# Expert pieces and convolution products in another order in the first and last steps, and no discarded products behind the first projection

## The reference

```python
x = x + _L0_conv_ref(_gn(x), g1, w_qkv, mem_kv, w_out, b_out, g2)
x = x + _L1_conv_ref(_gn(x), expert_weight, rconv_w, rconv_b, fc_w, fc_b)
```

## Time and profile before

| | us |
|---|---|
| median of the runs | 445.23 |
| the profiled execution | 443.4 |
| its span | 441.7 |
| TensorE busy | 417.4 (95%) |
| VectorE (DVE) busy | 350.1 (79%) |
| ScalarE (ACT) busy | 295.5 (67%) |
| GpSimd (POOL) busy | 264.9 (60%) |
| mean granted TensorE clock | 0.995 |

### The profile page before, as it was taken

The page is one execution under the profiler, slowest core; times in us unless marked ns, Lnnn a source line. Parts: engine busy times, 40 slices in busy tenths (PEclk is TensorE's granted clock), DMA queues, the critical chain, the costliest instruction groups (busy, mean ns, idle before and its releaser), DMA issues.

```text
span 441.7 us, 8932 instructions
## 1 busy us (share of the span) xinstructions
PE 417.4 (95%) x2638; PEld 368.5 (83%) x2638; DVE 350.1 (79%) x769; ACT 295.5 (67%) x907; POOL 264.9 (60%) x249
## 2 busy tenths in 40 slices
PE   7798898999999999999999999999999999999796
PEld 6698796989898988889887989888888989788585
DVE  3474989797989899797989798998979696967710
ACT  2766867868676868678676868686786868544221
POOL 4745648567584849396775849394956756424130
PEclk9999999999999999999999999999999999999899
DMA  6420242316262443515162524425161525242331
GB/s 190 181 96 2 95 192 96 131 62 237 98 235 98 159 176 125 211 45 229 64 240 95 219 113 148 185 96 236 42 229 62 192 95 192 95 174 113 158 128 47
DMA packets 18787, 61.63 MB, mean 140 GB/s; under 512 B 2992, under 2 KB 4032, under 8 KB 18752
## 3 DMA queue, kind: packets, MB, share of 16 engines
q1 hardware_dynamic: 18752, 61.21, 36.6%
HBM read 19.29 MB, written 8.39 MB: 63 GB/s over the span
## 4 chain that ended last, share of the span: by engine, by line
PE 48%; DVE 22%; issue 16%; ACT 10%; DMA 1%; POOL 1%; DVEq 1%; ACTq 0%; SPq 0%; POOLq 0%
PE ps_conv L1255 15%; PE ps_y L1200 6%; PE ps_att L1167 6%; DVE w_full L1006 4%; ACT expert_raw L655 4%; DVE y_scaled L894 3%; PE ps_y L1206 3%; PE ps_y L1190 3%; DVE route_terms L960 3%; ACT qk L594 3%; DVE q_exp L846 2%; PE ps_qkv L1146 2%; PE ps_qkv L1147 2%; PE ps_qkv L1148 2%; PE ps_stat L1213 2%
## 5 line engine op out<-in xcount | busy, mean ns | idle before, releaser
L594 ACT ACTIVATE qk<-ps_qkv,scale 128x256 f32<-128x256 f32 x128 | 55.5, 472 | 5.6 <-PE ps_qkv L1148 3.4
L537 POOL TENSOR_TENSOR left_hi<-zeros 128x32 fp32r<-128x32 f32 x16 | 7.5, 469 | 78.6 <-DMA right_lo<-img_lo 78.6
L661 ACT ACTIVATE w_hi<-w_full 128x1152 fp32r<-128x1152 f32 x16 | 18.7, 1168 | 51.1 <-DVE w_full L1012 51.1
L530 POOL TENSOR_TENSOR w_lo<-w_full,w_hi 128x1152 fp32r<-128x1152 f32 x16 | 42.8, 2675 | 11.2 <-ACT w_hi L661 6.2
L485 POOL TENSOR_TENSOR x_lo<-x,x_hi 128x1024 fp32r<-128x1024 f32 x16 | 38.4, 2400 | 14.4 <-ACT x_hi L584 14.4
L511 POOL TENSOR_TENSOR scale<-ssq,minus_half 128x8 f32<-128x8 f32 x16 | 26.2, 1639 | 32.5 <-DVE ssq L887 32.5
L1146 PE MATMUL ps_qkv<-wqk_hi,x_hi 128*128 128x256 f32 x128 | 40.8, 319 | 2.4 <-ACT x_nt L575 1.3
L635 ACT ACTIVATE y_scaled<-ps_y 128x128 f32<-128x128 f32 x128 | 33.5, 293 | 14.0 <-PE ps_y L1200 14.0
L1255 PE MATMUL ps_conv<-left_lo,w_hi 128*128 128x512 f32 (+1 forms) x96 | 39.1, 407 | 0.0
L1255 PE MATMUL ps_conv<-right_hi,w_lo 128*128 128x512 f32 (+1 forms) x96 | 38.5, 401 | 0.0
L1255 PE MATMUL ps_conv<-right_lo,w_hi 128*128 128x512 f32 (+1 forms) x96 | 37.9, 395 | 0.0
(11 more groups left out here) (152 smaller groups left out, 1333.9 us busy)
## 6 DMA issues: line engine op xcount, KB each, us to landing
xa<-in_x_dram SPq DMA_DIRECT2D x16, 512.0 KB, 4.0
xb<-in_x_dram SPq DMA_DIRECT2D x16, 512.0 KB, 4.6
out_dram<-expert_raw SPq DMA_DIRECT2D x16, 512.0 KB, 2.9
left_hi<-img_hi SPq DMA_DIRECT2D x16, 511.5 KB, 2.9
right_hi<-img_hi SPq DMA_DIRECT2D x16, 511.5 KB, 3.7
left_lo<-img_lo SPq DMA_DIRECT2D x16, 511.5 KB, 2.9
right_lo<-img_lo SPq DMA_DIRECT2D x16, 511.5 KB, 3.7
expert_raw<-_conv_expert_weight_dram SPq DMA_DIRECT2D x1, 1728.0 KB, 9.2
```

Source lines behind the costliest of these rows:

```text
L530: nc.gpsimd.tensor_tensor(w_lo[p][:, :, :].rearrange("p t o -> p (t o)"), w_full[:, :], w_hi[p][:, :, :].bitcast(F32).rearrange("p t o -> ...
L594: nc.scalar.activation(qk[:, t, :], ps_qkv[t % 2][:, 0:QK], ACT.Copy, scale=scale1[:, t:t + 1]).then_inc(qkv_done, 1)
```

## The change

Four things differ. `keep_busy` and its 126 products go, and `constants` issues two discarded products instead of four. The expert pieces go to other places in the lists of TensorE and ACT. The convolution of samples 1 to 14 goes by tap (three parts of one tap, then the next tap), with the waits for `w_lo`, `img_lo` and the borders before its first product, while samples 0 and 15 go by pass as before. And `conv_at` draws 4 products ahead of their place in step 4 and 12 in step 18.

```diff
@@ ACT step
                 do(results, t, p, 5, 0)
+                once(expert_evacuate, t, 2, 0)
+                once(expert_evacuate, t, 2, 1)
+                once(expert_evacuate, t, 2, 2)
+                once(expert_evacuate, t, 2, 3)
                 once(expert_evacuate, t, 3, 6)
-                once(expert_evacuate, t, 2, 3)
-                once(expert_evacuate, t, 2, 4)
+                once(expert_evacuate, t, 3, 7)
...
                 do(results, t, p, 5, 1)
+                once(expert_evacuate, t, 2, 4)
                 once(expert_evacuate, t, 2, 5)
                 do(k_x_evacuate, t, p, 2)
                 do(x_copy, t, p, 1, 1)
                 do(x_k_evacuate, t, p, 2)
-                once(expert_evacuate, t, 3, 7)
+                once(expert_evacuate, t, 3, 8)
                 do(q_evacuate, t, p, 2, 0)
                 do(qkv_evacuate, t, p, 1, 0)
-                once(expert_evacuate, t, 3, 8)
...
-                once(expert_evacuate, t, 1, 0)
                 do(squares2, t, p, 2)
-                once(expert_evacuate, t, 1, 1)
-                once(expert_evacuate, t, 1, 2)
@@ TensorE constants
-                discarded(4)
+                discarded(2)
@@ TensorE convolution
+                by_pass = isinstance(b, int) and b in (0, B - 1)
+                if by_pass:
+                    products = [(n, part) for part in range(3) for n in range(TAPS)]
+                else:
+                    products = [(n, part) for n in range(TAPS) for part in range(3)]
+                    pe.wait_ge(w_lo_done, b + 1)
+                    pe.wait_ge(img_lo_done, b + 1)
+                    pe.wait_ge(edges_done, b + 1)
                 for h in range(2):
                     if past(b, 1):
                         pe.wait_ge(result_done, 2 * (b - 1) + h + 1)
-                    for pass_ in range(3):
+                    for n, part in products:
@@ TensorE step
+                def conv_at(at, n):
+                    if isinstance(t, int) and t == at:
+                        conv(n)
...
                 conv(1)
-                once(expert_transpose, t, 2, 6)
                 conv(3)
-                once(expert_transpose, t, 3, 8)
                 conv(2)
-                keep_busy(t, "key_contexts")
                 do(key_contexts, t, p, 2)
...
                 do(key_context_transpose, t, p, 2)
+                conv_at(OLDEST + B - 2, 3)
                 turn(group_means, t, p, 0)
...
                 conv(1)
+                conv_at(OLDEST + B - 2, 5)
+                conv_at(OLDEST, 4)
                 if not isinstance(t, int) or t != 1:
                     turn(group_variances, t, p, 0)
...
-                once(expert_transpose, t, 1, 0)
-                once(expert_transpose, t, 1, 1)
                 do(outputs, t, p, 2)
-                once(expert_transpose, t, 1, 2)
+                conv_at(OLDEST + B - 2, 4)
                 do(routing, t, p, 3)
...
-                once(expert_transpose, t, 1, 3)
                 conv(6)
-                keep_busy(t, "project")
+                once(expert_transpose, t, 2, 6)
                 do(project, t, p, 1, 6)
                 conv(1)
                 do(project, t, p, 1, 7)
+                once(expert_transpose, t, 1, 0)
+                once(expert_transpose, t, 1, 1)
                 conv(5)
+                conv(1)
+                conv(14)
+                once(expert_transpose, t, 1, 2)
+                once(expert_transpose, t, 1, 3)
+                once(expert_transpose, t, 2, 7)
+                do(x_transpose, t, p, 0, 0)
+                do(x_transpose, t, p, 0, 1)
+                do(k_part_transpose, t, p, 1)
+                conv(8)
+                do(k_shift, t, p, 1)
+                once(expert_transpose, t, 2, 8)
                 once(expert_transpose, t, 1, 4)
                 once(expert_transpose, t, 1, 5)
...
                 do(y_transpose, t, p, 2)
                 conv(3)
```

More of the change, by code:

```diff
@@ L1237, in convolution @@
                         pe.wait_ge(result_done, 2 * (b - 1) + h + 1)
-                    for pass_ in range(3):
-                        if h == 0 and pass_ == 0:
+                    for n, part in products:
+                        if n == 0 and part == 0 and h == 0:
                             pe.wait_ge(w_hi_done, b + 1)
                             pe.wait_ge(img_hi_done, b + 1)
-                        if h == 0 and pass_ == 1:
+                        if by_pass and n == 0 and part == 1 and h == 0:
@@ L1243, in convolution @@
                             pe.wait_ge(img_lo_done, b + 1)
-                        if h == 0 and pass_ == 2:
+                        if by_pass and n == 0 and part == 2 and h == 0:
                             pe.wait_ge(w_lo_done, b + 1)
[L1246 to L1259, removed]
@@ new lines, in convolution @@
+                        if by_pass and n == KW and part == 0 and h == 0:
+                            pe.wait_ge(edges_done, b + 1)
+                        tap = TAP_ORDER[n]
+                        down = tap // KW - 1
+                        top, bottom = max(HH * h, -down), min(HH * (h + 1), H - down)
+                        hi, lo = ((left_hi, left_lo), (img_hi, img_lo), (right_hi, right_lo))[tap % KW]
+                        into = ps_conv[h][:, W * (top - HH * h):W * (bottom - HH * h)]
@@ L1261, in step @@
+                        weight, pixels = ((w_hi[p], hi[p]), (w_hi[p], lo[p]), (w_lo[p], hi[p]))[part]
+                        last = mm(into, weight[:, tap, :], pixels[:, top + down:bottom + down, :],
+                                  start=(n == 0 and part == 0), stop=(n == TAPS - 1 and part == 2))
+                        if n == TAPS - 1 and part == 2:
+                            last.then_inc(conv_ps, 1)
+                        yield
             def step(t, p):
@@ L1311, in step @@
                 do(project, t, p, 1, 7)
+                once(expert_transpose, t, 1, 0)
+                once(expert_transpose, t, 1, 1)
                 conv(5)
+                conv(1)
[9 more added lines that the diff above has]
+                once(expert_transpose, t, 2, 8)
                 once(expert_transpose, t, 1, 4)
                 once(expert_transpose, t, 1, 5)
[L1315 to L1324, removed]
-                do(k_shift, t, p, 1)
-                keep_busy(t, "y_transpose")
                 do(y_transpose, t, p, 2)
```

## The result

| | before | after |
|---|---|---|
| median of 15 runs each, side by side | 444.16 us (441.41 to 446.77) | 447.00 us (444.83 to 448.53) |
| ratio after / before, 95% interval | | 1.0052 [1.0030, 1.0073] |
| profiled execution, its own time | 443.40 us | 446.32 us |
| its span | 441.7 us | 444.6 us |
| its mean granted clock | 0.995 | 0.962 |

The change made the kernel slower by half a per cent, 2.3 us by the ratio. The forecast was 446.9 us.

The account below looks back on a forecast made before the run. TensorE, busy 95% of the span, was taken as the main bound, with DVE and ACT bounding parts. Terms -1.3 - 0.3 - 0.2 + 4.4 + 0.3 + 0.7 - 1.9 = +1.7 gave a median of 446.9 us, range 442.8 to 450.5.

Parts of the forecast that it names:

- pieces: First projection: moving three expert evacuations off ACT between the fourth and fifth projection tile ends it sooner, -1.3 us.
- discarded products: Constants: two fewer let the x transposes of sample 0 start sooner, gain ending at ACT's squares; -0.3 us.
- third step: ACT in the warm-up: one big expert evacuation leaves the place between x_k_evacuate and q_evacuate; -0.2 us.
- the clock: Warm-up: without idle products TensorE's granted clock falls and slows the work behind; +4.4 us, bounds 0 and 8.8.
- by tap: Samples 1 to 14: first convolution product waits for w_lo in two or three steps; +0.3 us, bounds 0 and 2.0.
- step 4: Four convolution products pulled ahead of group_variances and mixing, where TensorE is the bound; +0.7 us, bounds 0.2 and 0.9.
- the last step: From 407.7 us: 12 products fill TensorE's waits and avoid the clock fall, despite a w_lo wait; -1.9 us.
- All three stretches: Warm-up, 22.6 to 29.6, 42.5 to 49.6 and 64.0 to 70.5 us: become quiet; falls cost 1.6, 1.6, 1.2 us.
- The clock mostly holds: Warm-up rival: remaining real products keep the clock up, sum -2.7 to +0.1 us, likeliest 443.7 us; chance 0.22.
- Slow level lasts: Warm-up rival: low-clock spells last twice as long, 8.0 us for the three, giving 450.5 us; chance 0.15.
- w_lo late in every step: Loop rival: w_lo ends last in each step, costing 3.9 us instead of 0.3, giving 450.5 us; chance 0.05.
- No gain from reordering: First projection and last step rival: their -3.2 us shrinks to about -1, giving 449.1 us; chance 0.08.

Follow-up runs that it names:

- the fourth set: Kernel before without the 39 idle products ahead of project 6 (steps 2 and 3) and the x transposes of step 3; ratio 1.0012.
- the combined kernel: Kernel before with expert transposes and evacuations moved and 12 convolution products pulled ahead in step 18, all by pass, idle products kept; 439.96 us, ratio 0.9928.
- the second stretch: Kernel before without the 18 idle products between the x transposes of step 2 and the key contexts of sample 1; ratio 1.0037.
- the first stretch: Kernel before without the 38 idle products between the first x transposes of step 1 and the key contexts of sample 0; ratio 1.0046.
- the pieces: Kernel before with only the change's order of expert transposes and evacuations, 115 idle products kept, all by pass, four discarded; 442.83 us, ratio 0.9959.
- third: Kernel before without the 31 idle products between the x transposes of step 3 and the first convolution product; ratio 1.0030.

## Why the prediction was right

*The sum.* It gave +1.7 on the profiled execution; the profiled execution after is 446.32, +2.9. The ratio says +2.3. That 446.9 and the measured 447.0 lie so close has luck in it: the forecast added 1.8 us for the distance to a median of 445.23 from three runs, and with 15 that median was 444.16. Errors of the terms cancelled as well. In the traces the start gave 0.7 where the forecast had 1.8 (pieces, discarded products, third step), the clock cost 5.3 for 4.4, the loop gave back 0.7 where by tap was to cost 0.3, and step 4 and the last step came out as forecast.

*Clock.* The heaviest term, and the one with the sign. All three stretches fell, as the quiet stretch of before had let one expect. That it fell in the one profiled execution was partly luck, for in three other traces it doesn't (last section). Forecast +4.4, measured +4.75 and 4.8 by the two ways of taking the products out. The parts were 1.6, 1.6 and 1.2 by forecast, 2.0, 1.6 and 1.3 by medians. In the trace of the change they are 2.2, 2.3 and 0.8. The first covers most of the 16 key-context products (3.37 us for 1.95) and the work up to 33 us. The third costs 0.8 us here, 0.5 in the kernel with all idle products out, and 2.0 where it alone was quiet. It goes with how much of the spell is left behind y_transpose of sample 1, where TensorE is the bound: the clock is back 2.9, 2.5 and 5.5 us behind the start of that y_transpose. The Trainium skill (TensorE: Matmul & The Clock Gate, section "HAM oscillation — how this bites in real kernels") says that the cost is paid again at each quiet gap. The trace agrees for these three; the gap before 413 us fell in six traces and not in three, and the fourth set shows dips that cost 0.5 us at most, for there another engine is the bound.

*Pieces.* Forecast -1.3 and, with the third step, -1.5. Measured -1.8 with an interval of 1.1 to either side, and -1.21 at the key contexts in the combined kernel's trace, where both executions ran the projection at the full level. In the change ACT's fifth tile starts 0.35 us behind the end of the fourth, as said. In the change's own trace only -0.68 is left; its x transposes ran at the low level (0.93 us longer), and so they did in the change with the idle products back, which has -0.49. The -0.2 for ACT's third step was a term too many: in the combined kernel's trace outputs of sample 1 are 0.15 us further ahead (-1.21 to -1.36), and y_transpose of sample 1 is back at -1.25.

*Discarded products.* Forecast -0.3, measured between -1.3 and +1.5. This stays open; it is below what these runs can tell.

*By tap.* Forecast +0.3 with 2.0 as its end. There is one wait, 0.19 us, in the loop besides sample 14's 0.9, which the last step's term held. The loop as a whole gained 0.7 us in the trace of the change. By tap isn't needed for it: with all samples by pass the kernels of the second stretch and of the projection gain 0.7 and 1.0 us over the same steps, and by tap alone gains 0.2. In the change nearly all of it comes between the y_transposes of samples 5 and 6 (+5.42 to +4.68), where DVE waits for the input of a later sample, in before and in the change:

```profile
178.50 1.29 DVE L744 BATCH_NORM_STATS2 stats<-xa 128x6 f32<-128x512 f32 x2 [2.29 <-DMA xa<-in_x_dram]
183.12 1.28 DVE L744 BATCH_NORM_STATS2 stats<-xa 128x6 f32<-128x512 f32 x2 [1.50 <-DMA xa<-in_x_dram]
```

The work behind it in DVE's list, y_scaled included, shifts with it. The other traces follow this wait: with 2.1 to 2.4 us of it the offset of that step moves by at most 0.14, with 2.62 and 2.77 it grows by 0.25 and 0.47, and with 0.9 or less it shrinks by 0.7. So this is a matter of when a transfer lands in an execution, and what sets that wasn't tried. The forecast had no term for it.

*Step 4.* Forecast +0.7, found +0.73 at the outputs of sample 2, and 0.8 in the change with the idle products back. Whether it reaches the end stays open (above).

*Last step.* Forecast -1.9 in all; from y_transpose of sample 15 to the first product of sample 15 the offset goes from +4.73 to +2.81: -1.92. Its inner numbers hold too: routing 0.95 later by forecast, 0.93 in the trace; the wait for w_lo 1, found 0.90; for w_hi 1.5, found 1.36. But 1.6 of the 1.92 is the fall that the trace of before happened to have; against the two traces that have the last step of before and no fall, the term is -0.3.

*The rivals.* "The clock mostly holds" fell with the first page after. "Slow level lasts" was part right: in each of the kernels with one stretch quiet the low level lasts some 6.9 us, twice the 3.4 us at 413, and up to 13.6 us in the change. But the prices stay under twice the 1.6 (2.8, 2.1 and 2.0 us in those traces), and all three together cost 5.3 us in the change and 5.7 with all idle products out, where this rival had 8.0. "w_lo late in every step" fell with the by-tap kernel. "No gain from reordering" fell with the idle products put back. A gain was within reach (-0.6% with the idle products back), so the change is slower by the clock alone.

## What to carry to other kernels

Products that compute nothing can carry the clock: before taking them out, find for each stretch which engine is the bound behind it, because a fall cost 1.3 to 2.8 us where TensorE is (three of four sets here) and at most 0.5 us where it isn't. Fill a wait of TensorE with real products only where it waits anyway: in the last step, by pass, this gave 1.2 us beside the fall that was gone, and in step 4, without such waits, it put the outputs 0.7 us back. Before a single trace is the witness for a fall, look at a second one. A change with parts of both signs is worth splitting: all in all it was +2.3 us, and its two gaining parts alone are -3.2.

## What the runs showed of the hardware

*The level at the start differs between executions of one program.* In the profiled executions of before and of the combined kernel the x transposes and the first projection ran at the full level. In the change's, the low level covers 9 to 16 us (rows at the top), and the key contexts of sample 0 start 0.5 us later than in the combined kernel. In those of the kernels without idle products, by tap, of two discarded products, without the first stretch and without the projection's it lies on the first projection, and the key contexts of sample 0 come 2.8 to 3.0 us late. It lies there too in those of the pieces and of the change without step 4. The pieces and the combined kernel are the same code up to step 18, and their key contexts of sample 0 start 2.2 us apart. The stretch in the kernel without idle products:

```profile
16.00:22.00 6.00, 4.91 (x23) 0.53 0.00 1
```

By tap changes nothing before 80 us and has this too, so it is no effect of the edits. It fits most of the scatter of the runs: of 95 runs of before beside the experiments, 44 with a mean granted clock of up to 0.988 take 446.4 us on average and 51 with 0.992 and more take 443.5. The profiled one (0.995) is of the second heap; no run of before from the first heap was traced, so that the late spell makes the heap is argued from the size, 2.9 us, and the clock.

In the first microseconds the clock's rows say less than the work does. The eight discarded records take 1.72 us in before and 1.06 here, in the kernel without idle products, and the granted clock is given as 1.00 for both:

```profile
8.33 1.06 PE L1071 MATMUL ps_stat<-ones 128*128 128x128 f32 x8
```

The Trainium skill (TensorE: Matmul & The Clock Gate, section "What's actually happening") says that the number of products at the low level at a kernel's start varies from run to run. The traces agree, and add where the spell lies: late, in the projection, it costs 3 us. A median of such runs moves with the share of each heap, and two single traces can differ by 3 us for no reason in the code. That is why the offsets above are read from the same work to the same work and not from zero.

*The same quiet gap brings the fall in one execution and not in another.* The stretch before 413 us, the forecast's witness, brought it in the traces of before and of the kernels with the idle products out, two discarded, first, third and projection stretch. In by tap, in the pieces and in the second stretch it didn't, though in the last two the gaps are those of before. The second stretch's:

```profile
410.00:416.00 6.00, 3.78 (x17) 1.00 0.30 120
415.11 0.67 PE L1213 MATMUL ps_stat<-route_prod,rstd 128*128 128x256 f32 x2 [0.64 <-POOL rstd L464]
```

That execution had lost 2.1 us behind its second stretch and still ended at a span of 441.9 us, 0.2 above before: the fall gives 1.6 of it back and the loop 0.7. With the 12 products pulled ahead the stretch is at full clock in all five traces that have them. The three stretches of the warm-up fell in every trace in which they were quiet (the change, the change without step 4, all idle products out, and each alone). What decides it at 413 us wasn't tried.
